# Keys and values projected ahead of queries in every block, early maxima evenly spaced, later keys behind turns

## The chip, the cores and the metric

The kernel runs on one core of one Trainium2 chip. The metric is the device time of one execution in microseconds (us). The engines are TensorE (PE in the profile), VectorE (DVE), ScalarE (ACT), GpSimd (POOL) and SyncE (SP), which issues most of the DMAs.

## The reference

One transformer layer on x of 4 x 1024 x 256 in float32: attention with rotary positions, 16 query heads over 4 key/value heads of 16 dimensions, then a gated feed-forward part with integer weights, each followed by a residual and a layer norm.

```python
q, k, v = x @ wq, x @ wk, x @ wv            # 256 -> 16x16, 4x16, 4x16
q, k = rotate(q), rotate(k)                 # cos, sin by position
attn = softmax(q @ k.T / 4) @ v             # 4 query heads share a key/value head
x = layernorm(x + attn @ wo)
g, u = x @ dequant(gate_w).T, x @ dequant(up_w).T
x = layernorm(x + (silu(g) * u) @ dequant(down_w).T)
```

## The kernel before, in words

**Projections.** The 4096 tokens are eight blocks `m` of 512 (two per batch `b`, `c` is which). A block has six places, the hooks `h`, one group of float32 matmuls each: `project_q(m, j, k)` (L1315) for the two halves `j` of the query rows and two halves `k` of the contraction, then `project_kv` (L1324), which writes keys and values at once. Queries go to the two halves of `pair_bank0`. VectorE multiplies them by the cosine and sine tables (`rotary_q`, L789, two products per `j`), GpSimd adds (`rotate`, L585), ScalarE rounds to a high part (`high_part`, L1083), GpSimd or VectorE takes the low part (`low_of` L591, `low_first` L812), and SyncE stores both to DRAM (`store_q`, L397) to load them back in another layout (`load_q` L325, `load_k` L340). The keys of batch 0 take the same way at once (`rotary_k`, `rotate_k(0)`, `high_of_k`, `low_first_k`), with the difference of their two halves of positions made by one matmul (`make_gap`, L1342). Keys of batches 1 to 3 are only copied out (`copy_k_rows`, L1095) and rotated later by GpSimd (`products_k`, `rotate_k`, `high_of_k`, `low_of_k`, `gap_of`, L601 to L638). Values are copied (`copy_v_rows`), transposed on TensorE (`transpose_v`, L1296) and taken into `v_all` (`take_v`).

**Maxima ahead of scores.** The softmax subtracts a row maximum, which is found before the scores by extra matmuls (`max_block`, L1278) that VectorE reduces (`take_max`, L832). A pair of heads has four halves (`HALVES`) of 512 queries, a half has eight key tiles `t` (units `g = 8n + t`), a unit four maxima. `LEAD = 12` units of them are done ahead, as 24 early steps of two maxima placed at hooks of the projection blocks by `FIRST_STEP` (L256). Each two steps (four maxima) use `early_banks`; ScalarE clips two of them (`difference`, L1126) and VectorE reduces each with its partner (L844). When a half's last maximum is in, VectorE "turns" it: `row_maxima`, `shift_high` (L856), `shift_low` (L860), `turn_shift` (L866), and the result goes by 2 KB DMAs (L338) into rows of `q_sb`, which the scores need.

```python
 249  early = {(n, h): [] for n in range(BLOCKS) for h in range(HOOKS)}
 ...
 256      early[divmod(FIRST_STEP + i // 2 * (BLOCKS * HOOKS - FIRST_STEP) // LEAD, HOOKS)].extend(step(i))
```

**Attention.** Each unit: four score matmuls (L1431) for two exponentials (L1180), four or five maxima of 12 units later (L1286), and four matmuls with the values of the unit before (`pv`, L1372). Unit 0 is written out on its own. SyncE's program (L352 on) is one list in which every store and load waits in turn: `load_shift(0, 0)`, the eight DMAs that unit 0's scores wait for (L1426), stands behind `store_q(6, 0)` (L432 to L434).

Of the kernel before, what the change touches and what calls it, by code (L numbers as in the profile page):

```python
# [13 lines left out]
P = 128  # L14
# [40 lines left out]
FIRST_STEP = 28  # L55
VALUES_UNIT = 1
EARLY_BANKS = 4
LAG = 2
# [10 lines left out]
def layer(nc, x, xT, wq, wkv, wo, gate_w, gate_scale, up_w, up_scale, down_w, down_scale,  # L69
          cos, sin_q, cos_k, sin_k, identity, out):  # L70
    ctx = ExitStack()
    with ctx:
# [105 lines left out]


# [103 lines left out]
        for g in range(HALVES * PAIRS * KT):  # L283
            for key in loop_entries(g):
                half, e = key
                place(key, "above" if e < MAXES and blocks(half, e // 4)[e % 4][1] == 2 else "max")
            if g == VALUES_UNIT:
                place(("v", B - 1), "v")
# [63 lines left out]
        def _(sp):  # L352
# [13 lines left out]

            sp.dma_start(wq_sb[:], wq.rearrange("(k p) n -> p k n", p=P)).then_inc(wq_loaded, 16)
            load_x(0)
            load_q_tables(0)
            sp.dma_start(wkv_sb[:], wkv.rearrange("(k p) n -> p k n", p=P)).then_inc(wkv_loaded, 16)  # L370
            for dst, src in ((cosk_sb, cos_k), (sink_sb, sin_k)):
                sp.dma_start(dst[:], src).then_inc(k_tables_loaded, 16)
            load_x(1)
            load_q_tables(1)
            sp.dma_start(ident[:], identity).then_inc(ident_loaded, 16)
            for m in range(2, BLOCKS):
                load_x(m)
            def load_shift(pair, k):
# [5 lines left out]
            def first_queries():  # L384

                for slot in range(4):
# [20 lines left out]

# [9 lines left out]
            def projections(b, first, last):  # L417
                for c in range(2):
                    m = 2 * b + c
                    if last and c == 0:  # L420
                        load_kv(0, 0)
                        load_k(k_max, 0, 1, kmax_loaded, sp)
                        load_q(0, QH, sp)
                    if m == 2:
                        store_gap(0, (0,))
                        store_q(m, 0, (0,))
                        store_gap(0, (1,))
                        store_q(m, 0, (1,))
                        first_queries()
                        first_keys()  # L430
                    else:
                        store_q(m, 0)  # L432
                    if last and c == 0:
                        load_shift(0, 0)  # L434
                    store_q(m, 1)
                    if m == 4:
                        load_q(0, 1, sp)
                    if m == 1:
                        store_k(0)
# [17 lines left out]
            for dst, src in ((wo_sb, wo.rearrange("(k p) n -> p k n", p=P)), (gate_s, gate_scale),  # L457
                             (up_s, up_scale), (down_s, down_scale)):
                sp.dma_start(dst[:], src).then_inc(weights_loaded, 16)
# [30 lines left out]
            def attention(p, first, last):  # L490
                for k in range(HALVES):
# [4 lines left out]
                    if k == 0:  # L496
                        load_q(p, HALVES - 1, sp)
                    elif not last:
                        load_q(p + 1, k - 1, sp)
                    if k == 0:  # L500
                        if not first:
                            sp.wait_ge(pv_done, 8 * n)
                        load_kv(p, 1)
# [28 lines left out]
                    if first and k < B - 1:  # L532
                        bring_half(k + 1)
                        store_k(k + 1)
                    if k % QH == 0 and not last:
# [36 lines left out]
        def _(pool):  # L572
# [49 lines left out]
            def high_of_k(b):  # L622
                pool.wait_ge(k_rot_ready, b + 1)
# [16 lines left out]
            for m in range(BLOCKS):  # L640
                rotate(m, 0)
                rotate(m, 1)
                if m % 2 or m >= FIRST:
                    low_of(m, 0)
                low_of(m, 1)
                if m == 1:
# [136 lines left out]
        def _(dve):  # L783
# [5 lines left out]
            def rotary_q(m, j):  # L789

                cols = slice((m % 2) * CH, (m % 2 + 1) * CH)
                dve.wait_ge(proj_ready, 3 * m + j + 1)
# [4 lines left out]
                src = q_bank[j]  # L797
# [4 lines left out]
            def rotary_k():  # L802

                dve.wait_ge(proj_ready, 3 + 3)
# [87 lines left out]
            for m in range(BLOCKS):  # L892
# [4 lines left out]
                early_maxima(m, 0)  # L897
                rotary_q(m, 0)
                early_maxima(m, 1)
                early_maxima(m, 2)  # L900
                rotary_q(m, 1)
# [4 lines left out]
                if m == 1:  # L906
# [711 lines left out]
```

## Time and profile before

| what | us |
|---|---|
| median of 3 runs | 900.68 (899.43 to 904.11) |
| the profiled execution's own time | 900.83 |
| its span in the trace | 899.0 |
| PE busy | 881.1 (98%) |
| DVE busy | 746.0 (83%) |
| ACT busy | 712.5 (79%) |
| POOL busy | 267.6 (30%) |

Projections take the span up to 67 us, attention from there to about 680, the feed-forward part the rest. Busy times are sums over an engine's instructions. The chain that ended last is the profile's own walk back through who released whom; idle time of an engine off that chain costs nothing. Instructions of SyncE and DMA issues are not counted as busy; they are shown in the timeline as SPq and ACTq.

### The profile page before, as it was taken

What the parts mean: (1) busy time and instruction counts of PE and PEld (TensorE: products, weight loads), DVE (VectorE), ACT (ScalarE), POOL (GpSimd) and SP (SyncE); (2) the same over time, 40 slices, a digit from 0 to 9 for tenths busy, and PEclk for the clock granted to TensorE, in tenths of its full rate; (3) what the DMA queues carried; (4) which work ended last, traced back from release to release, by engine and by line L of the source; (5) the groups of instructions that cost most, each with busy time, mean ns of one, the idle gap of its engine ahead of it and who ended that gap; (6) DMA issues with size and microseconds to landing.
All of it is one profiled execution on the core that took longest, in us unless ns stands there. A gap on an engine that the chain in (4) does not pass through costs nothing.

```text
span 899.0 us, 16217 instructions
## 1 busy us (share of the span) xinstructions
PE 881.1 (98%) x5658; PEld 460.8 (51%) x5658; DVE 746.0 (83%) x1656; ACT 712.5 (79%) x929; POOL 267.6 (30%) x231
## 2 busy tenths in 40 slices
PE   9999999999999999999999999999999999999996
PEld 3334444444444444444444444444436888888885
DVE  5678999999999999999999999999955455665545
ACT  1457899999999999999999999999985565555564
POOL 6545340035434000001001000220104765665555
PEclk9998999999999999999999999999999999999998
DMA  9864554323343132332213313121111010110001
GB/s 333 260 150 133 117 125 88 90 82 76 94 122 68 45 77 56 57 77 68 52 46 93 73 45 80 44 60 37 39 54 51 31 48 24 48 47 25 24 24 48
DMA packets 53458, 69.98 MB, mean 78 GB/s; under 512 B 17344, under 2 KB 26560, under 8 KB 53376
## 3 DMA queue, kind: packets, MB, share of 16 engines
q1 hardware_dynamic: 50280, 65.53, 28.8%
q0 software_dynamic: 864, 3.15, 1.2%
q8 instruction: 46, 0.75, 0.4%
q10 hardware_dynamic: 2232, 0.25, 0.2%
q14 instruction: 36, 0.29, 0.1%
HBM read 46.74 MB, written 16.25 MB: 70 GB/s over the span
## 4 chain that ended last, share of the span: by engine, by line
PE 86%; DVE 8%; ACT 2%; issue 2%; DMA 1%; SPq 1%; ACTq 0%; POOL 0%; POOLq 0%; DVEq 0%
PE pv_bank L1372 24%; PE ring_bank L1286 22%; PE pair_bank L1503 13%; PE pair_bank L1431 12%; DVE block_max L848 4%; PE pv_bank L1529 3%; PE ring_bank L1529 3%; PE ring_bank L1382 3%; PE pair_bank L1320 2%; ACT probs L1180 1%; DVE above L844 1%; DMA q_sb<-shift 1%; PE ring_bank L1397 1%; PE pv_bank L1266 1%; PE pv_bank L1338 1%
## 5 line engine op out<-in xcount | busy, mean ns | idle before, releaser
L1180 ACT ACTIVATE probs<-pair_bank 128x1024 f32<-128x1024 f32 x512 | 496.0, 1023 | 43.6 <-PE pair_bank L1431 43.4
L848 DVE TENSOR_REDUCE block_max<-ring_bank 128x1 f32<-128x384 f32 x854 | 485.9, 608 | 16.9 <-PE ring_bank L1286 6.9
L1286 PE MATMUL ring_bank<-k_max,q_sb 48*128 48x512 f32 x1122 | 311.7, 442 | 2.8 <-DVE block_max L848 0.9
L1286 PEld LDWEIGHTS ring_bank<-k_max,q_sb 48*128 48x128 f32 x1122 | 150.2, 184 | 261.1 <-DVE block_max L848 116.0
L1372 PE MATMUL pv_bank<-probs,v_all 128*17 128x512 f32 x2048 | 270.6, 600 | 0.7 <-ACT probs L1180 0.7
L1431 PE MATMUL pair_bank<-q_sb,k_sb 50*128 50x512 f32 x1024 | 222.3, 428 | 2.0 <-ACT probs L1180 0.7
L1038 DVE SCALAR_TENSOR_TENSOR hid<-pair_bank,up_s,silu 128x512 f32<-128x512 f32 x63 | 47.1, 748 | 84.8 <-ACT silu L1245 84.8
L1431 PEld LDWEIGHTS pair_bank<-q_sb,k_sb 50*128 50x128 f32 x1024 | 99.5, 186 | 30.7 <-ACT probs L1180 7.6
L753 POOL TENSOR_TENSOR hid_l<-hid,hid_h 128x512 fp32r<-128x512 f32 x63 | 81.7, 1297 | 86.1 <-ACT hid_h L1224 85.4
L668 POOL TENSOR_TENSOR attn<-attn,inv_rows 128x1024 f32<-128x1024 f32 x7 | 16.7, 2383 | 301.3 <-DMA inv_rows<-inv_d 228.8
L844 DVE CUSTOM_DVE_ANT_0 above<-ring_bank,above 128x512 f32<-128x512 f32 x133 | 91.2, 687 | 7.5 <-ACT above L1126 7.1
L1126 ACT ACTIVATE above<-ring_bank 128x512 f32<-128x512 f32 x135 | 80.4, 598 | 6.6 <-PE ring_bank L1286 4.2
L1245 ACT ACTIVATE silu<-pair_bank,gate_s 128x512 f32<-128x512 f32 x63 | 43.0, 683 | 47.0 <-PE pair_bank L1503 47.0
L1224 ACT ACTIVATE hid_h<-hid 128x512 fp32r<-128x512 f32 x63 | 39.6, 629 | 41.7 <-DVE hid L1038 41.7
L1372 PEld LDWEIGHTS pv_bank<-probs,v_all 128*17 128x17 f32 x2048 | 34.1, 96 | 64.5 <-issue 63.6
L1503 PE MATMUL pair_bank<-x1T_h,gate_h 128*128 128x512 f32 x126 | 40.4, 402 | 0.0
L1503 PE MATMUL pair_bank<-x1T_l,gate_h 128*128 128x512 f32 x126 | 39.9, 398 | 0.0
L1503 PE MATMUL pair_bank<-x1T_l,up_h 128*128 128x512 f32 x126 | 39.7, 396 | 0.0
L1503 PE MATMUL pair_bank<-x1T_h,up_h 128*128 128x512 f32 x126 | 39.6, 396 | 0.0
L686 POOL TENSOR_SCALAR w_f<-w_raw 128x1024 f32<-128x1024 int32 x6 | 16.6, 2772 | 69.5 <-DVE shift L866 69.5
L1529 PE MATMUL pv_bank<-down_h,hid_h 128*128 128x256 f32 x128 | 33.6, 284 | 0.3 <-DVE v_all L987 0.3
L1529 PE MATMUL ring_bank<-down_h,hid_h 128*128 128x256 f32 x128 | 33.5, 284 | 0.0
(143 smaller groups left out, 869.0 us busy)
## 6 DMA issues: line engine op xcount, KB each, us to landing
k_max<-k_parts SPq DMA_DIRECT2D x96, 96.0 KB, 3.6
q_sb<-q_parts SPq DMA_DIRECT2D x64, 128.0 KB, 3.3
k_sb<-k_parts SPq DMA_DIRECT2D x96, 64.0 KB, 2.3
attn<-xT SPq DMA_DIRECT2D x8, 512.0 KB, 8.8
q_parts<-high SPq DMA_DIRECT2D x16, 256.0 KB, 3.7
q_parts<-low SPq DMA_DIRECT2D x16, 256.0 KB, 3.4
q_sb<-q_parts SPq DMA_DIRECT2D x64, 64.0 KB, 3.4
attn<-pv_sb SPq DMA_DIRECT2D x128, 32.0 KB
```

The lines of the kernel that those rows point to most:

```text
L753: pool.tensor_tensor(hid_l[:, it, :], hid[it % 2][:], hid_h[:, it, :].bitcast(fp32), ALU.subtract).then_inc(hid_l_ready, 1)
L844: dve.tensor_tensor_reduce(out=buf[:], in0=bank, in1=buf[:], scale=1.0, scalar=-3.0e38, op0=ALU.add, op1=ALU.max, accum_out=block_max[half ...
L848: dve.reduce_max(block_max[half % 2][:, col:col + 1], bank[:, 0:width], axis=AX.X).then_inc(ring_used, 1)
L1038: dve.scalar_tensor_tensor(out=hid[it % 2][:], in0=pair_bank[it % 2][:, 1, :], scalar=up_s[:, it:it + 1], in1=silu[it % 2][:], op0=ALU.mul ...
L1126: act.activation(above[(count - 1) % 2][:], bank_of(key), ACT.Relu).then_inc(above_ready, 1)
L1180: act.activation(probs[t % 2][:, 2 * pr:2 * pr + 2, :], pair_bank[pr][:], ACT.Exp, scale=D ** -0.5).then_inc(probs_ready, 1)
L1245: act.activation(silu[it % 2][:], pair_bank[it % 2][:, 0, :], ACT.Silu, scale=gate_s[:, it:it + 1]).then_inc(silu_ready, 1)
L1286: pe.matmul(bank[:, 0:last - first], q_sb[k][rows, i, qt * P:(qt + 1) * P], k_max[k // QH][rows, kind * CH + first:kind * CH + last], star ...
L1372: ins = pe.matmul(pv_bank[32 * j:32 * j + D + 1, :], v_all[:, head, t, 0:D + 1], probs[t % 2][:, 2 * (j % 2) + j // 2, :], start=(t == 0), ...
L1431: ins = pe.matmul(pair_bank[pr][:, r, :], k_sb[s][rows, t * P:(t + 1) * P], q_sb[k][rows, pr, :], start=True, stop=True)
L1503: ins = pe.matmul(pair_bank[it % 2][:, u, :], w[:, k, it * P:(it + 1) * P], v[c][:, k, :], start=(q == 0), stop=(q == len(terms) - 1))
L1529: ins = pe.matmul(sum_bank[t // 2][:, (t % 2) * E:(t % 2 + 1) * E], v[:, k, t * P:(t + 1) * P], w[:, k, :], start=(k == 0 and t % 2 == 0 a ...
```

## The change

- Each block's hooks run keys and values, then query half 0, then half 1. Consumers follow: `rotary_k` stands ahead of the queries of block 1, row copies in the same block, ScalarE's `high_part(m, j)` in block `m + 1`.
- `FIRST_STEP` is 24: early steps start in block 4 and stand at hooks 0, 2 and 4 of blocks 4 to 7.
- Values of batch `b` are transposed in block `2b + 1`, batch 3's too (before: in unit 1). The key difference is made at block 2's first place.
- The last query half, q(7, 1), is projected into `pv_bank`, and its rotary products stand within unit 0's maxima; scores of unit 0 wait for q(7, 0) alone. Its high parts go to units 2 and 3.
- SyncE loads `wkv` first, `wq` third, the last two blocks of x after the first keys; the other first loads move ahead by blocks; the scales are loaded later.
- GpSimd's `high_of_k(b)`, b from 1 on, waits for turn b.

```diff
-FIRST_STEP = 28
-VALUES_UNIT = 1
+FIRST_STEP = 24
+X_AHEAD = 6
...
+        def q_bank_of(m, j):
+            return pv_bank[:] if (m, j) == (BLOCKS - 1, 1) else q_bank[j]
...
             if b == 0:
-                early[2 * b + 2, HOOKS - 2].append(("gap", b))
-            if b < B - 1:
-                early[2 * b + 3, 1].append(("v", b))
+                early[2 * b + 2, 0].append(("gap", b))
+            early[2 * b + 1, 3].append(("v", b))
...
             def projections(b, first, last):
                 for c in range(2):
                     m = 2 * b + c
-                    if last and c == 0:
-                        load_kv(0, 0)
-                        load_k(k_max, 0, 1, kmax_loaded, sp)
-                        load_q(0, QH, sp)
-                    if m == 2:
+                    if m == 0:
+                        for part in range(2):
+                            store_q(m, 0, (part,))
+                            store_q(m, 1, (part,))
+                    elif m == 1:
+                        store_k(0)
                         store_gap(0, (0,))
                         store_q(m, 0, (0,))
                         store_gap(0, (1,))
+                        first_queries()
                         store_q(m, 0, (1,))
-                        first_queries()
                         first_keys()
+                        store_q(m, 1)
+                        for later in range(X_AHEAD, BLOCKS):
+                            load_x(later)
                     else:
+                        if last and c == 1:
+                            load_q(0, HALVES - 1, sp)
+                            load_kv(0, 1)
                         store_q(m, 0)
-                    if last and c == 0:
-                        load_shift(0, 0)
-                    store_q(m, 1)
+                        if last and c == 0:
+                            load_shift(0, 0)
+                        store_q(m, 1)
...
             def high_of_k(b):
+                after_turn(b)
                 pool.wait_ge(k_rot_ready, b + 1)
...
+                early_maxima(m, 0)
+                if m == 1:
+                    rotary_k()
+                early_maxima(m, 1)
+                if c and 1 < m <= FIRST:
+                    low_first(m - 1)
+                early_maxima(m, 2)
+                rotary_q(m, 0)
                 early_maxima(m, 3)
                 early_maxima(m, 4)
-                if m == 1:
-                    rotary_k()
-                if c == 0 and m < FIRST:
-                    low_first(m)
+                if m < BLOCKS - 1:
+                    rotary_q(m, 1)
                 early_maxima(m, 5)
...
+                    if n == 3 and g == 0:
+                        rotary_q(BLOCKS - 1, 1)
...
-            pe.wait_ge(parts_ready, Q_PARTS * BLOCKS)
+            pe.wait_ge(parts_ready, Q_PARTS * (BLOCKS - 1) + 2)
...
-                        if g == VALUES_UNIT:
-                            transpose_v(B - 1)
```

VectorE around the turn of half 0, in block 6. Of before, with `by_sin0` being the first product of q(6, 1), ahead of the turn:

```order
L800 TENSOR_TENSOR by_sin0<-pair_bank0,sinq_sb 128x512
L800 TENSOR_TENSOR by_cos1<-pair_bank0,cos_sb 128x512
L844 ISA above0,block_max0<-ring_bank1,above0 128x512
L844 ISA block_max0 128x1
L844 ISA above1,block_max0<-pair_bank1,above1 128x512
L844 ISA block_max0 128x1
L852 TENSOR_REDUCE row_max0<-block_max0 128x16
L856 CAST shift_rows0<-row_max0 128x16
L860 TENSOR_TENSOR shift_rows0<-row_max0,shift_rows0 128x16
L866 STREAM_TRANSPOSE shift0<-shift_rows0 128x32
```

Of the change, from the turn (L873 to L887) on:

```order
L873 TENSOR_REDUCE row_max0<-block_max0 128x16
L877 CAST shift_rows0<-row_max0 128x16
L881 TENSOR_TENSOR shift_rows0<-row_max0,shift_rows0 128x16
L887 STREAM_TRANSPOSE shift0<-shift_rows0 128x32
L821 TENSOR_TENSOR by_cos0<-pair_bank0,cos_sb 128x512
L821 TENSOR_TENSOR by_sin1<-pair_bank0,sinq_sb 128x512
L865 ISA above0,block_max1<-pair_bank1,above0 128x512
L865 ISA block_max1 128x1
L865 ISA above1,block_max1<-pair_bank1,above1 128x512
L865 ISA block_max1 128x1
L821 TENSOR_TENSOR by_sin0<-pair_bank0,sinq_sb 128x512
L821 TENSOR_TENSOR by_cos1<-pair_bank0,cos_sb 128x512
```

Both products of q(6, 0), an early step and then the products of q(6, 1) now stand behind the turn.

TensorE at the end of block 7 and the first scores. Of before:

```order
L1338 MATMUL pv_bank<-attn,wkv_sb 64x512
L1338 MATMUL ring_bank2<-attn,wkv_sb 64x512
L1286 MATMUL ring_bank0<-k_max0,q_sb1 128x512
L1286 MATMUL ring_bank1<-k_max0,q_sb1 128x512
L1286 MATMUL pair_bank1<-k_max0,q_sb1 128x512 x2
L1431 MATMUL pair_bank0<-q_sb0,k_sb0 128x512 x2
```

Of the change:

```order
L1343 MATMUL pv_bank<-attn,wq_sb 128x512
L1319 MATMUL ring_bank0<-ident,v_rows1 128x128 x4
L1343 MATMUL pv_bank<-attn,wq_sb 128x512
L1305 MATMUL ring_bank1<-k_max0,q_sb1 128x512
L1305 MATMUL pair_bank1<-k_max0,q_sb1 128x512 x2
L1305 MATMUL ring_bank0<-k_max0,q_sb1 128x512
L1454 MATMUL pair_bank0<-q_sb0,k_sb0 128x512 x2
```

The last values' transposes and the query projection into `pv_bank` stand directly ahead of the scores; keys and values of block 7 are done earlier.

## Rows read from the trace of the kernel before

**Rows 1.** Page: the chain that ended last, share of the span by engine
```profile
PE 86%; DVE 8%; ACT 2%; issue 2%; DMA 1%; SPq 1%; ACTq 0%; POOL 0%; POOLq 0%; DVEq 0%
```
**Rows 2.** Windows: stretch, length, busy (instructions) per engine, granted clock, DMA share, GB/s
```profile
66.90:71.20 4.30, 3.30 (x14) 1.45 (x12) 3.61 (x10) 4.30 (x8) 2.45 (x2) 0.98 0.41 122
71.20:77.60 6.40, 6.40 (x27) 3.46 (x28) 3.26 (x6) 4.27 (x9) 4.75 (x4) 0.50 0.56 151
77.60:93.20 15.60, 14.65 (x97) 6.01 (x96) 15.11 (x30) 11.99 (x14) 6.74 (x7) 0.99 0.52 139
120.00:200.00 80.00, 79.79 (x565) 33.31 (x561) 78.15 (x171) 74.51 (x90) 13.89 (x11) 1.00 0.40 93
```
**Rows 3.** Timeline of PE: start, us, operation, [idle before and its releaser]
```profile
11.85 3.70 PE L1320 MATMUL pair_bank<-attn,wq_sb 128*128 128x512 f32 x8
17.34 3.70 PE L1320 MATMUL pair_bank<-attn,wq_sb 128*128 128x512 f32 x8
22.85 1.02 PE L1347 MATMUL ring_bank<-rotated_k,key_signs 128*64 128x512 f32 x2
36.75 0.50 PE L1286 MATMUL pair_bank<-k_max,q_sb 48*128 48x512 f32 x2 [1.44 <-DMA k_max<-k_parts]
...
50.49 0.49 PE L1286 MATMUL pair_bank<-k_max,q_sb 48*128 48x512 f32 x1
51.15 1.98 PE L1320 MATMUL pair_bank<-attn,wq_sb 128*128 128x512 f32 x4
53.06 0.50 PE L1286 MATMUL pair_bank<-k_max,q_sb 48*128 48x512 f32 x1
54.74 0.49 PE L1286 MATMUL pair_bank<-k_max,q_sb 48*128 48x512 f32 x1
56.13 0.64 PE L1338 MATMUL ring_bank<-attn,wkv_sb 128*64 128x512 f32 x1
...
67.41 0.50 PE L1431 MATMUL pair_bank<-q_sb,k_sb 50*128 50x512 f32 x2 [0.34 <-DVE by_cos L800]
73.18 1.11 PE L1300 MATMUL ring_bank<-ident,v_rows 128*128 128x128 f32 x4
```
**Rows 4.** Timeline of DVE
```profile
18.18 2.84 DVE L810 TENSOR_TENSOR k_by_sin<-ring_bank,sink_sb 32x512 f32<-32x512 f32 x4
55.56 0.69 DVE L800 TENSOR_TENSOR by_sin<-pair_bank,sinq_sb 128x512 f32<-128x512 f32 x1
57.98 0.08 DVE L844 DVE_READ_ACCUMULATOR2_ANT block_max<- 128x1 f32 x1
59.11 0.21 DVE L866 STREAM_TRANSPOSE shift<-shift_rows 128x32 f32<-128x32 f32 x1
68.22 0.68 DVE L844 CUSTOM_DVE_ANT_0 above<-pair_bank,above 128x512 f32<-128x512 f32 x1
82.83 1.21 DVE L856 CAST shift_rows<-row_max 128x16 fp32r<-128x16 f32 x1
```
**Rows 5.** Timeline of POOL, then lines L856 and L860 alone: duration in ns, least, median, most
```profile
56.33 2.51 POOL L589 TENSOR_TENSOR rotated<-by_cos,by_sin 128x512 f32<-128x512 f32 x2 [5.60 <-DVE by_sin L800]
82.73 1.28 POOL L629 TENSOR_TENSOR low_k<-rotated_k,high_k 128x512 fp32r<-128x512 f32 x1
...
L856 DVE CAST shift_rows<-row_max x32: 163/164/1207, 58.3 to 653.6; 128x16 fp32r<-128x16 f32 x32
...
L860 DVE TENSOR_TENSOR shift_rows<-row_max,shift_rows x32: 163/165/1145, 58.9 to 653.8; 128x16 fp32r<-128x16 f32 x32
```
**Rows 6.** Timeline of SP: issues, start and us; last row, PE at a later half
```profile
29.89 2.69 SPq L347 DMA_DIRECT2D k_max<-k_parts  x6
...
61.32 4.47 SPq L338 DMA_DIRECT2D q_sb<-shift  x8
...
280.65 0.72 ACTq L338 DMA_DIRECT2D q_sb<-shift  x1
284.04 0.70 PE L1431 MATMUL pair_bank<-q_sb,k_sb 50*128 50x512 f32 x3 [0.31 <-DMA q_sb<-shift]
```

More of the change, by code:

```diff
@@ L365, in load_q_tables @@
                     sp.dma_start(dst[:, cols], src[:, cols]).then_inc(q_tables_loaded[c], 16)
+            sp.dma_start(wkv_sb[:], wkv.rearrange("(k p) n -> p k n", p=P)).then_inc(wkv_loaded, 16)
+            load_x(0)
             sp.dma_start(wq_sb[:], wq.rearrange("(k p) n -> p k n", p=P)).then_inc(wq_loaded, 16)
-            load_x(0)
             load_q_tables(0)
-            sp.dma_start(wkv_sb[:], wkv.rearrange("(k p) n -> p k n", p=P)).then_inc(wkv_loaded, 16)
+            load_x(1)
             for dst, src in ((cosk_sb, cos_k), (sink_sb, sin_k)):
                 sp.dma_start(dst[:], src).then_inc(k_tables_loaded, 16)
-            load_x(1)
             load_q_tables(1)
             sp.dma_start(ident[:], identity).then_inc(ident_loaded, 16)
-            for m in range(2, BLOCKS):
+            for m in range(2, X_AHEAD):
                 load_x(m)
@@ L384, in first_queries @@
             def first_queries():
-                for slot in range(4):
+                for slot in range(2):
                     sp.wait_ge(stored[slot], 16 * 2)
@@ L456, in _, with load_scales @@
             swap_strips(1)
-            for dst, src in ((wo_sb, wo.rearrange("(k p) n -> p k n", p=P)), (gate_s, gate_scale),
-                             (up_s, up_scale), (down_s, down_scale)):
-                sp.dma_start(dst[:], src).then_inc(weights_loaded, 16)
+            def load_scales():
+                for dst, src in ((wo_sb, wo.rearrange("(k p) n -> p k n", p=P)), (gate_s, gate_scale),
+                                 (up_s, up_scale), (down_s, down_scale)):
+                    sp.dma_start(dst[:], src).then_inc(weights_loaded, 16)
             def store_pv(pair, k):
@@ L496, in attention @@
                     if k == 0:
-                        load_q(p, HALVES - 1, sp)
+                        if not first:
+                            load_q(p, HALVES - 1, sp)
                     elif not last:
@@ L534, in attention @@
                         store_k(k + 1)
+                    if first and k == 1:
+                        load_scales()
                     if k % QH == 0 and not last:
@@ L1136, in _ @@
                 b, c = divmod(m, 2)
-                if c == 0 and b:
-                    if b > 1:
-                        copy_k_rows(b - 1)
-                    copy_v_rows(b - 1)
-                early_takes(m, 0)
-                early_takes(m, 1)
                 if m == 2:
                     high_of_k()
-                early_takes(m, 2)
-                early_takes(m, 3)
+                early_takes(m, 0)
                 if m == 2:
                     gap_high()
-                if m < BLOCKS - 1:
-                    high_part(m, 0)
-                early_takes(m, 4)
-                if m < BLOCKS - 1:
-                    high_part(m, 1)
-                early_takes(m, 5)
-            copy_k_rows(B - 1)
+                if m:
+                    high_part(m - 1, 0)
+                early_takes(m, 1)
+                if c:
+                    if b:
+                        copy_k_rows(b)
+                    copy_v_rows(b)
+                early_takes(m, 2)
+                if m:
+                    high_part(m - 1, 1)
+                for h in range(3, HOOKS):
+                    early_takes(m, h)
             def split_x1T(m, c):
@@ L1316, in project_q @@
                 i = 2 * m + j
-                if k == 0 and i >= 2:
+                if k == 0 and i == 0:
+                    pe.wait_ge(wq_loaded, 16)
+                if k == 0 and (m, j) == (BLOCKS - 1, 1):
+                    pe.wait_ge(v_rows_ready, B)
+                elif k == 0 and i >= 2:
                     before, which = divmod(i - 2, 2)
                     pe.wait_ge(parts_ready, Q_PARTS * before + 2 + 2 * which)
-                ins = pe.matmul(q_bank[i % 2], wq_sb[:, k, j * P:(j + 1) * P], x_in[m][:, k, :], start=(k == 0), stop=(k == KE - 1))
+                ins = pe.matmul(q_bank_of(m, j), wq_sb[:, k, j * P:(j + 1) * P], x_in[m][:, k, :], start=(k == 0), stop=(k == KE - 1))
                 if k == KE - 1:
@@ L1352, in _ @@
                     j, k = divmod(h, KE)
-                    if j < 2:
-                        project_q(m, j, k)
+                    if j == 0:
+                        project_kv(m, k)
                     else:
-                        project_kv(m, k)
+                        project_q(m, j - 1, k)
                     if m or h:
```

45 lines of the change are left out of this document (20 added, 25 removed).

## The prediction

> **What bounds the kernel now.** I read the page's chain first: 86% of it is TensorE [rows 1]. The windows then show where TensorE has company: in a stretch of the steady attention it is busy 79.79 of 80 us and VectorE 78.15 [rows 2], so neither has room, and nothing in the change alters what a unit costs there. What can move is the start. The timelines of the five queues up to 93 us are therefore read next, for three things: where TensorE waits during the projections, what the first scores at 67.41 wait for, and what happens right behind them. There the clock granted to TensorE falls from 0.98 to 0.50 of full, its lower level of 1.2 GHz, for 6.4 us, after a stretch in which it was busy 3.30 of 4.30 us; then VectorE is busy 15.11 of 15.60 us while it catches up [rows 2].
>
> The change keeps all matmuls. So the forecast is the shift of the first scores, plus what unit 0 and its followers gain or lose.
>
> **The projections' own pace.** A block of projections costs 5.49 us (11.85 to 17.34), the key difference 0.95, an early step of four maxima 0.66 (50.49 to 51.15), two query matmuls between steps 1.91 [rows 3]. Before, the first maxima waited 1.44 us for the first keys, and where two such steps stand at adjacent hooks the second took 1.39 instead of 0.66 (54.74 to 56.13) [rows 3]; the old spacing has four such pairs of hooks, which makes 4 x 0.73 = 2.9 us. At every other place each step has a free bank: its last maximum leaves VectorE 2.5 us after its first matmul (53.06 to 55.56, the next instruction) and the next step comes 0.66 + 1.91 = 2.57 later [rows 3, 4]. So this cost goes.
>
> The first keys: block 1's keys are ready 3.6 us earlier, since its four query matmuls (3.6 of the 3.70 shown) now come after them [rows 3]. The rotation of these keys (about 3.5 us, of it 2.84 in the row) now holds VectorE ahead of block 1's queries [rows 4], and GpSimd, ScalarE and the stores follow 3 to 4 us ahead of before. SyncE's six key loads ended at 32.58 and TensorE went on at 36.75, 4.2 us later [rows 3, 6]; with much the same issues ahead of them they should end near 28.8, which gives 33.0 at the latest, and rather less, since two 512 KB loads of x no longer share the queues. TensorE wants them after four and a third blocks: 6.5 + 4 x 5.49 + 0.95 + 1.1 for two transposes (half of what those of unit 1 take at half the clock) + 1.9 = 32.4. The wait of 1.44 shrinks to 0.2 (ends 0 and 1.4).
>
> Down the blocks, the step that completes half 0 (eighth of twelve, hook 2 of block 6) begins at 6.5 + 6 x 5.49 + 0.95 + 1.6 for three transposes + 7 x 0.66 + 3.7 for its block's own matmuls + 0.2 + about 1.1 for the changes between kinds of matmul (1.91 against 1.8, some ten times) = 51.6. Its last maximum is then reduced at 54.1; before, at 58.06 [rows 4]. Up to here the change gains some 4 us.
>
> **What is late next: unit 0's shift rows.** The scores need half 0's maxima as rows of `q_sb`, brought by eight DMAs that SyncE issues only after both stores of q(6, 0). Before: first product of q(6, 1) begun at 55.56 and done at 56.2, GpSimd's two additions 56.33 to 58.84, low part, store, eight issues from 61.32 to 65.79 [rows 4 to 6]. After, VectorE has the turn ahead of these products: step at 51.6, reduced at 54.1, turn 1.3 (57.98 to 59.32) gives 55.4, two products of q(6, 0) 1.2, the next early step 1.2, first product of q(6, 1) 0.6, done at 58.4. Then additions 2.5, low part 1.25, store 0.6, and the eight issues run from 62.8 to 67.3: 1.5 us **later** than before, although the turn itself is 4 us earlier. From the last issue's end to the scores there were at most 67.41 - 65.79 = 1.62 us; at a later half it was 284.04 - 281.37 = 2.67 [rows 6]. I take 1.5, nearer to the row of the same place: the scores start at 68.8, **+1.4 us** (ends: 64.9, when TensorE is there, which is -2.5, and 67.3 + 2.67 = 70.0, which is +2.6).
>
> TensorE itself would be there by 64.9: 51.6 + 0.7 + 1.9 + 0.7 + 1.9 = 56.8 for block 7's keys, the step behind them held to 58.5 by VectorE's queue after the turn, then 1.9 + 0.7 + 1.9 + 0.5 of transposes, some 0.7 until ScalarE has copied the last values, and 0.7 for the last step. It then stands idle for 4 us. Before, it waited 0.34 for q(7, 1) at this place [rows 3]; that wait goes, and this one replaces it.
>
> **Behind the first scores.**
> - Batch 3's transposes leave unit 1, where they took 1.11 us at the low clock, 1.0 of it before the next matmul [rows 3]: **-1.0** (ends -0.5, their time at full clock, and -1.0).
> - VectorE carried an early step's leftovers to 68.9 (68.22 + 0.68), 1.5 us into unit 0; in the changed kernel they are done during the idle time. Added are q(7, 1)'s two products, 1.2 us [rows 4]: **-0.3**. What waits for them is the first values' matmul of unit 1 only.
> - The clock: 6.4 us at half cost 3.2 [rows 2]. With 4 us of idle time ahead I expect the fall again, but its first part lies under the wait, where nothing is lost: **-1.0** (ends -3.2, no fall, and +3.2, twice as long).
> - GpSimd's keys. VectorE's cast in the turn of half 1 took 1.21 us against a median of 0.164, ending as GpSimd's low part did (82.73 to 84.01) [rows 4, 5]; the subtraction at L860 has a longest of 1.145 against 0.165. The gate puts `high_of_k(1)` behind the turn, but low(7, 1) (now after unit 3's second exponential, about 82) and then `products_k(1)` come to the same place. I take **0** (ends -2.0 and 0).
> - The Trainium skill's GPSIMD Engine Reference, section Specifications, says that GpSimd's SBUF interfaces are shared with VectorE's, for ops with two SBUF inputs or in a two-port mode. By that rule the gate would be worth the 2.0 us if nothing else of GpSimd's came there, and the cast's row agrees with it.
> - Loads of scales, x blocks 6 and 7, and the early q and k loads: hidden. Blocks 6 and 7 are issued near 31 and needed at 46; if that cover went, a block would wait as long as the load is late.
> - Steady attention and feed-forward: 0, same instructions.
>
> Sum: 1.4 - 1.0 - 0.3 - 1.0 = -0.9 against the profiled execution's 900.83 (span 899.0 and 1.8 around it), which stands 0.15 above the median of 900.68. Forecast: 900.68 - 0.9 = **899.8 us**.
>
> **Rivals.**
> 1. *The shift rows are in time.* If VectorE's queue in block 6 is 2 us shorter than I add up, or the stores overlap more, the scores start nearer 64.9: -2.5, -0.5 to -1.0, -0.3, and -3.2 if TensorE, no longer waiting, keeps its clock. This gives 894.2 to 896.9, say 895.5. For it: all the early gains are real by the rows. Against it: the order on VectorE and SyncE is fixed.
> 2. *VectorE is the bound of the catch-up.* It was busy 15.11 of 15.60 us up to 93.2 [rows 2], so what TensorE saves in units 0 to 3 is waited out again: only the later start (+1.4) and VectorE's own -0.3 count. 901.8 us.
> 3. *Slower: the idle time costs the clock twice over.* TensorE's 4 us of idle time before the first scores leaves it at 1.2 GHz for two stretches of 6.4 us in place of one: +3.2 in place of -1.0, 904.0; with the later half's landing time (2.67 in place of 1.5) 905.2. It decides once the wait is much longer than the short ones that came before the fall now, 1.0 us in 4.30 [rows 2]. The Trainium skill, TensorE: Matmul & The Clock Gate, Part 1, holds that the clock is throttled by default and activity releases it; that speaks against a change that makes one long wait out of many short ones. The trace agrees as far as the fall at 71.2 goes.
>
> **How the numbers follow.** The forecast has 0.50 (its own range 897 to 902), rival 1 0.22, rival 2 0.20, rival 3 0.08. About 0.5%, or 4.5 us, is what a measurement of this kernel tells from no change. Faster by more (under 896.2): most of rival 1 and a sliver of the forecast, 0.19. Slower by more (over 905.2): the far part of rival 3 and mishaps like late keys, 0.06. Within: 0.75. The range 895.0 to 904.0 leaves out the best of rival 1 and the worst of rival 3.
>
> **What would show it.** Right: no wait over 0.5 us at the first maxima, now at 32 to 33; early steps of 0.66; the turn of half 0 near 55; eight shift issues from 62 to 63; an idle of about 4 us before the first L1454, put down to the DMA of the shift; the clock at 0.50 around it; the cast of turn 1 still near 1 us. Wrong: first scores before 67, a clock that stays at 1.00, or a first maximum that waits over a microsecond. If VectorE's busy stretch that ends at 93.2 now ends within 1.5 us of it, the rest follows.

## The result, and the profile after

The changed kernel takes **901.95 us** (median of 20 executions, 899.57 to 906.66) against 899.40 us for the kernel before beside it (20 executions, 896.81 to 904.11): ratio 1.0031, 95% interval 1.002 to 1.0043. So it is some 2.5 us slower, where 0.9 us less was forecast. The profiled execution took 903.28 us (span 901.5), 2.45 above that of before.

The page's chain hardly differs from that of [rows 1]: TensorE holds 85% of it. New is who holds up the scores:

```profile
PE 879.4 (98%) x5658; PEld 459.7 (51%) x5658; DVE 743.4 (82%) x1655; ACT 713.0 (79%) x929; POOL 269.1 (30%) x232
...
PE 85%; DVE 5%; issue 2%; DMA 2%; ACT 2%; SPq 2%; POOL 1%; ACTq 0%; POOLq 0%; DVEq 0%
...
L1454 PE MATMUL pair_bank<-q_sb,k_sb 50*128 50x512 f32 x1024 | 223.2, 430 | 5.8 <-DMA q_sb<-shift 4.3 <-ACT probs L1203 0.6
```

TensorE's timeline of the changed kernel, which answers to [rows 3] (columns: start us, us, engine, line, operation, in brackets the idle time before and who ended it):

```profile
33.54 0.46 PE L1305 MATMUL pair_bank<-k_max,q_sb 48*128 48x512 f32 x1 [1.67 <-DMA k_max<-k_parts]
...
57.91 1.11 PE L1305 MATMUL pair_bank<-k_max,q_sb 48*128 48x512 f32 x2 [0.27 <-DVE block_max L865]
...
64.80 0.39 PE L1305 MATMUL ring_bank<-k_max,q_sb 48*128 48x512 f32 x1
69.24 0.79 PE L1454 MATMUL pair_bank<-q_sb,k_sb 50*128 50x512 f32 x2 [4.04 <-DMA q_sb<-shift]
...
73.79 0.79 PE L1305 MATMUL ring_bank<-k_max,q_sb 48*128 48x512 f32 x1 [1.26 <-DVE block_max L865]
```

The first keys are waited for 1.67 us (1.44 before), the early steps then run without the old stalls, TensorE is through at 65.2, and it stands idle for 4.04 us until the scores at 69.24 (67.41 before). In unit 0 it waits once more, 1.26 us, for VectorE.

VectorE's timeline (rows that answer to [rows 4]), with half 0's turn from 54.64 to 56.07, the products of q(6, 1) behind it, and those of q(7, 1) inside unit 0:

```profile
55.86 0.21 DVE L887 STREAM_TRANSPOSE shift<-shift_rows 128x32 f32<-128x32 f32 x1
...
58.38 0.69 DVE L821 TENSOR_TENSOR by_sin<-pair_bank,sinq_sb 128x512 f32<-128x512 f32 x1
...
71.85 0.68 DVE L821 TENSOR_TENSOR by_sin<-pv_bank,sinq_sb 128x512 f32<-128x512 f32 x1
72.45 0.68 DVE L821 TENSOR_TENSOR by_cos<-pv_bank,cos_sb 128x512 f32<-128x512 f32 x1
73.05 0.68 DVE L865 CUSTOM_DVE_ANT_0 above<-ring_bank,above 128x512 f32<-128x512 f32 x1
...
87.82 0.38 DVE L877 CAST shift_rows<-row_max 128x16 fp32r<-128x16 f32 x1
```

SyncE's timeline: the last store of q(6, 0), and behind it the eight shift DMAs, which end at 67.94 ([rows 6]: they ended at 65.79):

```profile
62.91 0.52 SPq L406 DMA_DIRECT2D q_parts<-low  x1
63.47 4.47 SPq L339 DMA_DIRECT2D q_sb<-shift  x8
```

Up to here, but for the waits at the first keys and in unit 0, the trace is the prediction to within 0.7 us. The windows are not. The last three stretches are those of [rows 2], the first is the low stretch but for its two ends (columns: stretch, busy time and instructions of PE, PEld, DVE, ACT, POOL, then the clock granted to TensorE, DMA share, GB/s):

```profile
67.20:87.00 19.80, 16.50 (x65) 8.00 (x66) 11.32 (x22) 10.30 (x14) 5.11 (x5) 0.50 0.38 97
```

```profile
66.90:71.20 4.30, 1.96 (x8) 1.41 (x8) 0.70 (x3) 1.13 (x2) 0.00 (x0) 0.50 0.47 140
71.20:77.60 6.40, 5.14 (x19) 1.97 (x18) 5.27 (x10) 3.23 (x4) 2.49 (x2) 0.50 0.50 116
77.60:93.20 15.60, 15.60 (x87) 7.33 (x83) 11.43 (x25) 11.31 (x15) 5.97 (x5) 0.69 0.34 85
```

The clock falls at 66.9, in the idle time, and stays at 0.50 (1.2 GHz) until 87.4: 20.5 us. Before, it was low for 6.8 us, a little more than the 6.4 of the window in [rows 2]:

```profile
71.00:77.80 6.80, 6.62 (x27) 3.68 (x28) 3.62 (x9) 4.67 (x9) 4.95 (x4) 0.50 0.56 152
```

From 77.6 to 93.2 TensorE is now busy 15.60 of 15.60 us and VectorE 11.43, where before it was VectorE that was full (15.11) [rows 2]. TensorE at its lower level has become the bound of the very stretch in which VectorE should have been it. VectorE's transpositions of the turns show where the difference arises:

| start of L887 (before: L866), us | half 0 | half 1 | half 2 | half 5 |
|---|---|---|---|---|
| before | 59.11 | 87.03 | 107.12 | 163.67 |
| after | 55.86 | 90.21 | 109.11 | 165.66 |
| after minus before | -3.25 | +3.18 | +1.99 | +1.99 |

A gain of 3.25 us turns into a loss of 3.18 between the two turns, and from half 2 on nothing more happens.

### The profile page after: what moved, and what is told of

Same layout as the page of the kernel before. It is cut to its first block, busy times and chain, and to the rows that moved or that the text cites. A ratio compares the mean times of both kernels' runs of the same rounds, so it can differ in the third digit from the quotient of the medians.

```text
span 901.5 us, 16211 instructions
## 1 busy us (share of the span) xinstructions
PE 879.4 (98%) x5658; PEld 459.7 (51%) x5658; DVE 743.4 (82%) x1655; ACT 713.0 (79%) x929; POOL 269.1 (30%) x232
## 4 chain that ended last, share of the span: by engine, by line
PE 85%; DVE 5%; issue 2%; DMA 2%; ACT 2%; SPq 2%; POOL 1%; ACTq 0%; POOLq 0%; DVEq 0%
PE pv_bank L1395 26%; PE ring_bank L1305 23%; PE pair_bank L1454 13%; PE pair_bank L1524 12%; PE pv_bank L1550 3%; PE ring_bank L1550 3%; PE ring_bank L1405 2%; DVE block_max L869 2%; ACT probs L1203 1%; PE pair_bank L1343 1%; DMA ident<-identity 1%; PE ring_bank L1420 1%; DMA q_sb<-shift 1%; DMA k_max<-k_parts 1%; DVE above L865 1%
## 5 line engine op out<-in xcount | busy, mean ns | idle before, releaser
L865 DVE CUSTOM_DVE_ANT_0 above<-ring_bank,above 128x512 f32<-128x512 f32 x128 | 88.1, 688 | 5.3 <-ACT above L1151 5.2
L1151 ACT ACTIVATE above<-ring_bank 128x512 f32<-128x512 f32 x140 | 83.2, 598 | 8.5 <-PE ring_bank L1305 5.8
L707 POOL TENSOR_SCALAR w_f<-w_raw 128x1024 f32<-128x1024 int32 x6 | 16.6, 2774 | 69.3 <-DVE shift L887 69.3
```

The costliest lines, as they stand in the source:

```text
L865: dve.tensor_tensor_reduce(out=buf[:], in0=bank, in1=buf[:], scale=1.0, scalar=-3.0e38, op0=ALU.add, op1=ALU.max, accum_out=block_max[half ...
L1151: act.activation(above[(count - 1) % 2][:], bank_of(key), ACT.Relu).then_inc(above_ready, 1)
```

## The clock differs from execution to execution

Each execution lists the mean granted clock of its core. The 20 of the changed kernel fall into groups: eleven at 0.991 to 0.993 have times of 899.57 to 902.19, two at 0.989 have 903.06 and 903.31, and seven at 0.985 or 0.986 have 902.53 to 906.66. The one profiled (0.986) is of the last group. The mean over the 20 is 0.9892, and over the 28, 33 and 33 executions of before in the three sets that follow 0.9941, 0.9934 and 0.9935 (for before's own 20 no clock is on record). Over all kernels measured here, taking each kernel's own mean out (244 executions), 0.001 less clock goes with **0.63 us** more. This is a correlation, and less than the 0.90 us of TensorE's time that 0.001 of 900 us is. The Trainium skill, TensorE: Matmul & The Clock Gate, section Terms, prices throttled time as its length times (1 - K/N), half of it here, which is that 0.90. The runs give less; that some of the slow time lies in waits or under VectorE's work and costs nothing would explain it, but is not shown.

The changed kernel's mean clock is some 0.0045 below that of before in those sets, which by this slope stands for 2.8 us, as much as the kernels differ by. But the clock is a consequence of something, and the experiments ask of what.

## The experiments

**Theory A**: the 4 us of idle time before the first scores cost their length and a longer low clock as well. **Theory B**: the later start and VectorE, which bounds the catch-up, make the difference, and the clock only coincides. **Theory C**: the spacing of the early steps is a cost or gain of its own. Each kernel is the changed one but for the edit shown; each ratio is against before, measured beside it on the same chip. There are three such sets, on three chips, and before itself has 898.87, 899.42 and 900.23 us in them: kernels of different sets are compared by their ratios.

**The changed kernel again** (after_again). No edit.

> The changed kernel itself, to have it beside the others on one chip. Theory A (the idle time before the first scores costs twice, by its length and by the low clock behind it): 901 to 903 us, with the clock low for about 20 us from 66.9 on. Theory B (the later start and VectorE's catch-up cost it, the clock only coincides): the same.

902.35 us, ratio 1.0035 [1.0022, 1.0047]. The same 4.04 us of idle time, but the clock fell twice, for 6.8 us each time (at 69.3 and 89.8), the second time out of a stretch in which TensorE was all but never idle:

```profile
69.90:75.90 6.00, 5.03 (x19) 2.11 (x18) 5.28 (x10) 3.61 (x5) 2.50 (x2) 0.50 0.60 163
76.60:90.20 13.60, 13.10 (x83) 5.37 (x81) 13.21 (x27) 11.52 (x15) 6.33 (x5) 0.99 0.37 97
90.80:95.80 5.00, 5.00 (x22) 2.67 (x23) 2.79 (x5) 2.34 (x3) 4.92 (x5) 0.50 0.60 187
```

At 90.80 to 95.80 TensorE is busy all the time at half the clock, with VectorE at 2.79 of 5.00. Half 1's turn came at 86.62, 3.6 us earlier than in the first trace, half 2's at 109.20, no earlier: the second fall took it back. Between the falls VectorE is busy 13.21 of 13.60 us, so in this execution it may have bound that part of the catch-up, as theory B has it.

**The shift first** (shift_first), which takes the idle time away:

```diff
-                        store_q(m, 0)
                         if last and c == 0:
                             load_shift(0, 0)
+                        store_q(m, 0)
                         store_q(m, 1)
```

> Edit: SyncE issues the eight shift DMAs of half 0 ahead of the stores of q(6, 0) instead of behind them. The turn is at 56.1, so they should be issued from about 58.6 to 63.1 and land by 64.8; the first scores come at 65.2 without a wait over 0.5 us. Theory A: the start moves 4 us ahead and the clock stays up, or falls for some 6 us as before the change: 2 to 4 us more come back, 894 to 896.5 us, below both kernels. Theory B: only the start's 4 us or less, 898 us or above.

898.84 us, ratio 1.0001 [0.9989, 1.0014]. Without the idle time the scores start 3.3 to 3.9 us earlier, and the time is 3.5 below the changed kernel beside it. That is about the idle time's length and no more, and lies in theory B's range (898 or above), not in A's (894 to 896.5). TensorE now runs into VectorE's queue, which still has early maxima and q(7, 1)'s products:

```profile
65.34 0.50 PE L1454 MATMUL pair_bank<-q_sb,k_sb 50*128 50x512 f32 x2
65.68 0.33 PE L1305 MATMUL ring_bank<-k_max,q_sb 48*128 48x384 f32 x1
67.19 0.49 PE L1305 MATMUL ring_bank<-k_max,q_sb 48*128 48x512 f32 x1 [1.18 <-DVE block_max L865]
...
70.61 0.79 PE L1305 MATMUL ring_bank<-k_max,q_sb 48*128 48x512 f32 x1 [1.33 <-DVE block_max L865]
```

The clock falls behind these waits as well (6.00 us at 0.50 from 69.00 in the windows), and its mean over the 11 executions is 0.9908, nearer to the changed kernel's 0.9898 than to before's 0.9941. A's first half (idle time costs) holds; its second, that without the idle time the clock would be as before, does not on the mean. In the profiled execution it does: the clock was low for 6.8 us, as before, half 2's turn came at 104.09 against 107.12, and the time was 898.08 against 900.83.

**Work in the wait** (fill_wait): four float32 matmuls whose result nobody reads, ahead of unit 0's scores.

```diff
+            pe.wait_ge(k_rows_ready, B - 1)
+            for n in range(4):
+                pe.matmul(ring_bank[2][:], wq_sb[:, 0, 0:P], x_in[BLOCKS - 1][:, 0, :], start=True, stop=True)
+
             pe.wait_ge(parts_ready, Q_PARTS * (BLOCKS - 1) + 2)
```

> Edit: four extra float32 matmuls (3.4 us) into a free bank between the last early step and the first scores, so that TensorE is busy while it waits; the shift DMAs are as late as in the changed kernel. First scores still at about 69.2. Theory A: the clock does not fall at 66.9, and the time is 2 to 5 us below the changed kernel, 897 to 900. Theory B: the time is that of the changed kernel, within 1 us.

900.37 us, ratio 1.0015 [1.0004, 1.0025], 2.0 us below the changed kernel beside it, with **more** work on TensorE and the scores at 68.33 (68.60 beside it). The mean clock over the executions is 0.9943, against 0.9898 of the changed kernel and 0.9941 of before.

```profile
64.22 3.70 PE L1386 MATMUL ring_bank<-attn,wq_sb 128*128 128x512 f32 x8
68.33 0.50 PE L1458 MATMUL pair_bank<-q_sb,k_sb 50*128 50x512 f32 x2 [0.41 <-DMA q_sb<-shift]
...
72.07 0.49 PE L1305 MATMUL ring_bank<-k_max,q_sb 48*128 48x512 f32 x1 [1.07 <-DVE block_max L865]
```

```profile
62.00:73.40 11.40, 9.45 (x40) 4.54 (x42) 7.95 (x20) 5.37 (x10) 3.79 (x3) 1.00 0.43 125
74.00:76.20 2.20, 2.20 (x14) 1.08 (x7) 0.97 (x3) 1.03 (x2) 0.00 (x0) 0.50 0.44 118
```

The low stretch is 3.4 us long here, from 73.4 to 76.8. This is the run that separates clock from wait: no dependence was taken away, and of waits only the idle time, which was made busy (VectorE's wait in unit 0 is still 1.07). By theory B alone a filler can't help, so B is not the whole of it; the 900.37 is 0.4 above the range that A had for it.

**q(7, 1)'s products ahead of unit 0's maxima** (rotary_first), in the idle time:

```diff
+                    if n == 0 and g == 0:
+                        rotary_q(BLOCKS - 1, 1)
...
-                    if n == 3 and g == 0:
-                        rotary_q(BLOCKS - 1, 1)
```

> Edit: VectorE's two products of q(7, 1) stand ahead of unit 0's maxima instead of after the third entry, so they run in VectorE's own idle time before the first scores. In the changed kernel TensorE waits 1.26 us for VectorE in unit 0. Theory A and B both: that wait shrinks to 0.1 to 0.4, 1 us less in all (900.5 to 901.5); if it is nothing, later units absorb what TensorE wins in unit 0, which speaks for VectorE as the bound (B).

899.92 us, ratio 1.0013 [1.0, 1.0025].

```profile
69.26 0.80 PE L1454 MATMUL pair_bank<-q_sb,k_sb 50*128 50x512 f32 x2 [4.05 <-DMA q_sb<-shift]
...
72.62 1.64 PE L1454 MATMUL pair_bank<-q_sb,k_sb 50*128 50x512 f32 x4
```

Idle time 4.05 and first scores at 69.26 as in the changed kernel, but the wait of 1.26 us in unit 0 is gone, and 2.0 (by the ratios) to 2.4 us of time with it; the mean clock is 0.9915. So this wait, which the sum did not have, was worth its length and perhaps some clock, and with it gone the kernel still stands 1.2 us above before.

**Without the gate on GpSimd's later keys** (no_gate): `after_turn(b)` removed.

> Edit: the changed kernel without GpSimd's wait for turn b in high_of_k(b). In its trace high_of_k(1) starts at 93.67 while turn 1 is over at 90.4, so the wait holds nothing there. Theory A and B: the same time as the changed kernel, within 1 us (901 to 903). If the gate is what costs, or what saves, it is off by more than that.

903.52 us, ratio 1.0041 [1.0022, 1.0061]. One of the ten executions took 1978.75 us; the ratio leaves it out, as does the mean clock below, and the median without it is 902.90. Against the changed kernel's 1.0035 nothing can be told. Half 1's turn did meet GpSimd's work:

```profile
82.56 1.00 DVE L876 CAST shift_rows<-row_max 128x16 fp32r<-128x16 f32 x1
...
84.89 1.16 DVE L880 TENSOR_TENSOR shift_rows<-row_max,shift_rows 128x16 fp32r<-128x16 f32 x1
```

But what it met were `low(7, 1)` and `products_k(1)`; `high_of_k(1)` ran at 90.22, when the turn (86.57) was over. In the changed kernel's first trace the cast took 0.38 and `high_of_k(1)` ran at 93.67, behind the turn at 90.21. In its second trace, where the clock was up at this place, the two took 0.99 and 1.16, as without the gate, and `high_of_k(1)` ran at 90.33, behind the turn at 86.62. So there too the gate held nothing. It was worth 0 in both, as the sum had it.

**Early steps at the old places** (step28): `FIRST_STEP = 28`.

> Edit: the changed kernel with FIRST_STEP 28 again, so the early steps start at hook 4 of block 4 and some stand at adjacent hooks; half 0 is then turned one place later, behind q(6, 0)'s products and directly ahead of q(6, 1)'s. Theory A (what matters is when the shift rows of unit 0 land and whether TensorE idles for them): TensorE arrives some 2 us later at the first scores, the products of q(6, 1) come no later than before, so the idle time shrinks from 4 us to 1 to 3 us and the time is 899 to 901. Theory C (the even spacing is worth 3 us by itself and is only hidden): slower than the changed kernel by 1 to 3 us, 903 to 905.

900.19 us, ratio 1.0003 [0.9991, 1.0016]: 2.5 us below the changed kernel's first ratio, 2.9 below its second.

```profile
68.80 0.80 PE L1454 MATMUL pair_bank<-q_sb,k_sb 50*128 50x512 f32 x2 [2.64 <-DMA q_sb<-shift]
```

TensorE's last step ends 1.0 us later than in the first trace and the idle time before the scores is 2.64 instead of 4.04, with the start at 68.80 (68.60 and 69.24 in the changed kernel's two traces); the mean clock is 0.9923. The early gain of the even spacing had gone into idle time, which is not neutral.

**The shift first, and steps at the old places** (shift_step28), both edits:

> Edit: shift_first with FIRST_STEP 28, the old spacing. Here the first scores wait for no shift rows in either spacing, so this prices the spacing alone. Theory C's 3 us: 901 to 902.5. If the first keys' wait and the gaps only move (VectorE is full from block 4 on anyway), 898.5 to 900.

900.71 us, ratio 1.0006 [0.9992, 1.0019], scores at 65.19, waits of 1.49 and 1.48 in unit 0. The time lies between the two ranges that were forecast. By the ratios the old spacing costs 0.5 us (1.0001 above, with overlapping intervals), far from theory C's 3, so C has nothing beyond the idle time that can be told from scatter.

**The shift first, q(7, 1)'s products one place later** (shift_rot_late): `if n == 4 and g == 0`, and a second time (shift_rot_late_again); **or in unit 1** (shift_rot_unit1): `if n == 1 and g == 1`.

> Edit: shift DMAs ahead of the stores of q(6, 0), as in shift_first, and VectorE's two products of q(7, 1) one entry later in unit 0 (after the fourth). In shift_first TensorE waited 1.18 and 1.33 us for VectorE in unit 0. If the second of these is the price of where the products stand, 0.5 to 1.3 us come back and the time is 897.5 to 898.3; if VectorE's total work is what bounds units 0 to 8, nothing comes back: 898.8.

> The same kernel as the one with the first shift ahead of q(6,0)'s stores and the last rotary products behind the fourth maximum's place in unit 0 (898.92, ratio 0.9987 [0.9974, 1.0]), a second time on another chip job. If it is really a little faster than the kernel before, the ratio is 0.998 to 0.9995 again (898 to 899.2); if the first was scatter, 1.000 to 1.001.

> The first shift ahead of q(6,0)'s stores, and the two rotary products of q(7,1) moved out of unit 0 to the second maximum's place of unit 1. TensorE's wait of 1.3 us near 70.6 leaves unit 0. If the place of these 1.2 us on VectorE matters (theory B): 1 us below the kernel with only the shift moved, some 898, since the products stand where four maxima have already been handed on. If VectorE only moves its lateness (theory A's reading of the runs so far): the same wait of 1 to 1.4 us stands in unit 1 or 2, and the time is 898.5 to 899.5.

898.92 (0.9987 [0.9974, 1.0]), 899.42 (0.9992 [0.9978, 1.0006]) and 899.15 us (0.9991 [0.9974, 1.0007]). In the last one the wait of 1.3 us went from unit 0 and did not come up in unit 1, which is what theory B said. Its 899.15 us lie in theory A's range, but before took 900.23 beside it: by the ratios it is 0.9 us below the kernel with only the shift moved, which is B's 1 us, with overlapping intervals. By their ratios all three are 3.5 to 4.3 us below the changed kernel. Against before they are at most 1 us better, with three intervals that all reach 1.0, so none is shown to beat both.

**The shift later still** (shift_late), behind both stores of q(6, 1):

> The changed kernel with the eight DMAs of the first shift moved once further back, behind both stores of q(6,1) too (its low part is ready at 64.97 in the trace of the changed kernel, so the eight DMAs start near 65.6 instead of 63.5). All agree: first scores at 71.1 to 71.4, TensorE idle about 6.0 us before them instead of 4.04. Theory A (idle time there costs its length and low clock behind it): 3 to 4 us above the changed kernel, some 905 to 906, and the low stretch behind the scores is longer. Theory B (VectorE bounds the catch-up, the clock is coincidence): 0 to 2 us above it, 902 to 904.

904.42 us, ratio 1.0052 [1.0034, 1.007].

```profile
72.19 0.80 PE L1454 MATMUL pair_bank<-q_sb,k_sb 50*128 50x512 f32 x2 [6.11 <-DMA q_sb<-shift]
```

2.07 us more of idle time cost 1.5 to 1.9 us by the ratios, about their length and not twice it, and the mean clock is 0.9895, as in the changed kernel. This is the range of B (0 to 2 us above the changed kernel) and speaks against A as I had put it: the price in clock does not grow with the idle time.

**The shift first, with the filler** (shift_fill):

> The first shift ahead of q(6,0)'s stores, and four float32 matmuls of 128 columns x 512 into an unused bank ahead of unit 0's scores, some 1.9 us of TensorE work where it has no idle time to fill. Theory A: the clock falls behind the scores all the same for VectorE's waits of units 0 and 1, and the filler costs its length, 900 to 901 (1.2 to 2 us over the kernel with only the shift moved), or, if VectorE gets ahead in these 1.9 us and TensorE's waits of units 0 and 1 go (2.7 us together), the clock stays at 1.00 there and the time is 896.5 to 898.5. Theory B: 898.5 to 899.5, since the filler only takes the place of these waits.

900.33 us, ratio 1.001 [0.9994, 1.0026], scores at 68.47, mean clock 0.9942. The four matmuls take 3.70 us (each in two passes, x8 in the row above), not the 1.9 I wrote. They put the scores 3.1 us later than without them and cost 0.8 us by the ratios, whose intervals overlap. Of what came back, 1.0 is the first wait in unit 0 (1.18 with the shift first, 0.19 here); the rest goes with the clock, which is again as high as before's.

**All of them in one table.** The last column but one adds up two things only: the first scores' start against the 67.41 of before, and 0.63 us for each 0.001 by which the mean clock lies under that of before in the same set. The fourth gives how long the clock was low behind the first scores, or from just before them on, in the one execution that was profiled; in before's trace it was 6.8, in the changed kernel's first one 20.5.

| kernel | idle before scores | first scores | low clock in the trace, us | mean clock | start + clock, us | measured (ratio x 899), us |
|---|---|---|---|---|---|---|
| after_again | 4.04 | 68.60 | 6.8 and 6.8 | 0.9898 | 1.2 + 2.7 = 3.9 | 3.1 |
| shift_first | 0 | 65.34 | 6.8 | 0.9908 | -2.1 + 2.1 = 0.0 | 0.1 |
| fill_wait | 0.41 | 68.33 | 3.4 | 0.9943 | 0.9 - 0.1 = 0.8 | 1.3 |
| rotary_first | 4.05 | 69.26 | 10.2 | 0.9915 | 1.9 + 1.6 = 3.5 | 1.2 |
| no_gate | 4.04 | 68.00 | 10.2 and 6.8 | 0.9884 | 0.6 + 3.2 = 3.8 | 3.7 |
| step28 | 2.64 | 68.80 | 10.2 | 0.9923 | 1.4 + 0.7 = 2.1 | 0.3 |
| shift_rot_late | 0 | 65.23 | 10.2 | 0.9902 | -2.2 + 2.0 = -0.2 | -1.2 |
| shift_step28 | 0 | 65.19 | 10.2 | 0.9908 | -2.2 + 1.6 = -0.6 | 0.5 |
| shift_late | 6.11 | 72.19 | 10.2 | 0.9895 | 4.8 + 2.5 = 7.3 | 4.7 |
| shift_rot_late_again | 0 | 65.10 | 13.7 | 0.9905 | -2.3 + 1.9 = -0.4 | -0.7 |
| shift_rot_unit1 | 0 | 65.77 | 10.2 | 0.9920 | -1.6 + 0.9 = -0.7 | -0.8 |
| shift_fill | 0 | 68.47 | 3.4 | 0.9942 | 1.1 - 0.4 = 0.7 | 0.9 |

Where the scores hardly wait, the two account for the time within 1.1 us. Where TensorE waits 2.6 us or more, the time is up to 2.6 below the sum: VectorE works off its queue meanwhile, and part of the low clock lies in the wait; that is my reading and no run separates the two. The start is itself uncertain: four traces (both of the changed kernel, rotary_first and no_gate), whose programs are the same up to the first scores, have it at 69.24, 68.60, 69.26 and 68.00.

## Why the prediction was wrong

The forecast was -0.9 us and the result +2.5, inside the range and beyond its sign. Step by step:

- **The projections' pace: right.** Early steps of 0.66 us, one stall of 0.27 instead of four of 0.73; turn of half 0 done at 56.07 (predicted 55.4), first product of q(6, 1) begun at 58.38 and done at 59.1 (58.4 predicted), TensorE through at 65.2 (64.9).
- **First keys: missed.** 0.2 us predicted, 1.67 measured, past the end of 1.4 and over the microsecond that stood among the signs of being wrong. It moved the following steps, the turn and so the shift by some tenths; most of what TensorE lost here it would otherwise have waited for at the scores.
- **First scores: right in kind, short in size.** Issues 63.47 to 67.94 (62.8 to 67.3 predicted), 1.30 us of landing (1.5), idle time 4.04 (4), start 69.24 (68.8): +1.8 in place of +1.4 in this trace (+1.2 in the second one).
- **VectorE behind the scores: a step that failed, at nothing in the sum.** The text said that only the first values' matmul of unit 1 waits for q(7, 1)'s products. They stand between two maxima of unit 0, and the next maximum's bank is freed behind them: 1.26 us, which cancels the -1.0 of the transposes and part of the -0.3. With the products moved away it was gone, and 2.0 us of time with it. This is rival 2's point, at one place.
- **The clock: the main step that failed.** I took -1.0, since "its first part lies under the wait, where nothing is lost". That was true of 2.3 us (66.9 to 69.24) and said nothing of how long the low level lasts behind them: 18.2 us in this trace. (The 3.2 us that it started from were those of a window; the whole stretch of 6.8 us cost 3.4.) What it cost can be read in three ways, which agree in sign alone. By difference in the profiled pair: 1.99 at half 5's turn, less 1.83 for the start and 1.26 for the wait, plus the 1.0 and 0.3 of the gains, is +0.2, or +0.7 with the 2.45 at the end. By making the idle time busy: 2.0 us came back, 0.3 of it from an earlier start, so +1.7. By the mean clocks of all executions: +2.8. So the term was off by 1.2 to 3.8 us. The first reading is small, as I take the windows, since part of TensorE's slowness took the place of waits for VectorE, which before was full:

Both traces' windows from 84 to 88 us, of before:

```profile
84.00:88.00 4.00, 3.05 (x19) 1.36 (x20) 4.00 (x10) 2.17 (x3) 2.48 (x3) 1.00 0.44 121
```

and of the changed kernel:

```profile
84.00:88.00 4.00, 4.00 (x21) 1.81 (x17) 2.53 (x6) 3.05 (x6) 2.34 (x2) 0.57 0.51 131
```

- **GpSimd's gate: right**, 0. The cast near 1 us that was to show it came in the second trace (0.99), not in the first (0.38).

Neither failed step makes the difference alone: without VectorE's wait the kernel still stands 1.2 us above before, with the idle time filled 1.3.

Rival 2 had 901.8, 0.15 from the median, and its number is right by luck in part: it left the clock out and had VectorE full behind the scores, which was so between the falls of the second trace and not in the first (11.43 of 15.60).

Rival 3 (4 us of idle time cost the clock twice over, 904.0) had the mechanism and the sign, and a chance of 0.08. Its size was too large for the median (901.95) and near the seven executions of the lowest clock (902.53 to 906.66). Its condition was not quite the right one: with the idle time removed the mean clock was still 0.9908, and with half as much again it was no lower. What brought it back to before's level was the filler, in both kernels that had it. Rival 1 had the scores at 64.9 and 895.5 us; with the scores at 65.34 the time was 898.84, as VectorE's waits in unit 0 and the clock kept the rest. Its range was also added up wrongly: its terms give 893.7 to 897.4, not 894.2 to 896.9.

**What stays open.** Why the low stretch is 20.5 us in one execution of the changed kernel and 6.8 in another, and why the clock fell a second time at 90 us in the latter, isn't settled: up to the first scores the two traces show the same instructions and the same 4.04 us of idle time. Nor can start, waits and clock be told apart below about 1 us, as the three readings above show.

## What to carry to other kernels

Work that is moved earlier gains nothing if the chain behind it doesn't move, and the idle time that it leaves on TensorE is not neutral: check which issue or store the next wait hangs on (here eight DMAs behind two stores) before moving anything ahead of it. Where TensorE must wait some microseconds in front of a dense stretch, a few dummy matmuls in the wait are worth a try (2.0 us of 902 here), but only where there is a wait: without one the same four gained nothing (0.8 us more by the ratios, within scatter). Read the mean clock of every execution beside its time; the one that is profiled may lie at either end.

## What the runs showed of the hardware

- The granted clock stayed at its lower level while TensorE was busy without a break: 15.60 of 15.60 us from 77.6 to 93.2 in the changed kernel, 9.8 us of it at the lower level, and 5.00 of 5.00 in its second trace. The Trainium skill, TensorE: Matmul & The Clock Gate, Part 1, says that activity releases the throttle; here the trace does not agree: TensorE was busy and the level stayed low for those 9.8 us, and it fell anew out of 13.10 busy us in 13.60.
- One kernel on one core has several clock levels from execution to execution (0.985 to 0.993), and they go with some 4 us of time (medians of 900.97 for the eleven quicker clocks, 905.17 for the seven slowest).
- TensorE went on 1.28 to 1.30 us after the last of the shift's eight issues ended, in each of the seven traces in which it waited for them (1.30 in the changed kernel: 67.94 to 69.24). Of the two times in [rows 6], 2.67 is such a wait at a busier place, and 1.62 only an upper bound, since TensorE waited for VectorE there.
